# One sequence's start made on chip, another table of work for it, and fixed PSUM banks in a transformer block on one core

## What is computed

```python
xn = layernorm(x)
# attention: 16 heads of 16 channels, q = k = v = xn, causal
w = softmax(where(causal, q @ k.T / sqrt(16), min))
attn = w @ v
# ffn: lora rows from tokens 1..16 of the sequence itself
m1 = (even[:, :4, :, None] * odd[:, :4, None, :]).reshape(B, 1024, 256)
m2 = (even[:, 4:, :, None] * odd[:, 4:, None, :]).reshape(B, 256, 1024)
h = gelu(xn @ W1.T + scale * (xn @ m1.T) + b1)
ffn = h @ W2.T + scale * (h @ m2.T) + b2
out = x + attn + ffn
```

## Time and profile before

| | |
|---|---|
| median of 3 runs | 940.79 us (940.0 to 941.72) |
| profiled execution | 942.08 us |
| its span | 940.3 us |
| TensorE matmul busy | 855.6 us (91%) |
| ScalarE busy | 682.3 us (73%) |
| VectorE busy | 621.6 us (66%) |
| GpSimd busy | 185.3 us (20%) |
| chain that ended last | TensorE 72%, ScalarE 16%, VectorE 4%, DMA 2% |

### The profile page before, as it was taken

The page is one execution under the profiler, slowest core; times in us unless marked ns, Lnnn a source line. Parts: engine busy times, 40 slices in busy tenths (PEclk is TensorE's granted clock), DMA queues, the critical chain, the costliest instruction groups (busy, mean ns, idle before and its releaser), DMA issues.

```text
span 940.3 us, 17554 instructions
## 1 busy us (share of the span) xinstructions
PE 855.6 (91%) x7040; PEld 485.9 (52%) x7040; DVE 621.6 (66%) x1260; ACT 682.3 (73%) x737; POOL 185.3 (20%) x264
## 2 busy tenths in 40 slices
PE   1689999999999999999999999999999999999994
PEld 1255645656465554646446564555646555465642
DVE  7876695767677596675957668576767759562511
ACT  0547688777878778776887778777787877878782
POOL 1202122120312213121221212212121211212120
PEclk9989999999999999999999999999999999999998
DMA  4845436462373723555353633646246383313113
GB/s 134 298 137 169 144 101 192 130 184 74 102 213 113 241 64 114 145 167 187 102 164 84 203 123 103 191 139 175 73 114 201 114 241 91 107 35 93 38 12 101
DMA packets 212145, 127.18 MB, mean 135 GB/s; under 512 B 139168, under 2 KB 180320, under 8 KB 211040
## 3 DMA queue, kind: packets, MB, share of 16 engines
q1 hardware_dynamic: 212064, 126.06, 45.6%
HBM read 84.02 MB, written 42.01 MB: 134 GB/s over the span
## 4 chain that ended last, share of the span: by engine, by line
PE 72%; ACT 16%; DVE 4%; DMA 2%; issue 2%; POOL 2%; SPq 1%; DVEq 0%; ACTq 0%
PE o_ps L458 27%; PE work L486 15%; PE work L473 14%; PE scores L438 14%; ACT probs L394 13%; ACT L404 2%; POOL probs L386 2%; PE work L498 2%; ACT gelu L404 1%; DMA even<-even_dram 1%; DVE acc L670 1%; DVE xt_w L632 1%; DVE w_lo L599 1%; DMA q_dram<-xt_pair 0%; DMA xn<-x 0%
## 5 line engine op out<-in xcount | busy, mean ns | idle before, releaser
L394 ACT ACTIVATE probs<-scores 128x1024 f32<-128x1024 f32 x576 | 553.5, 1025 | 160.1 <-PE scores L438 159.9
L386 POOL TENSOR_SCALAR_AFFINE_SELECT probs<-probs 128x512 f32<-128x512 f32 x256 | 182.8, 732 | 735.6 <-ACT probs L394 735.6
L458 PE MATMUL o_ps<-probs,v_ones 128*32 128x512 f32 (+3 forms) x3072 | 281.0, 493 | 1.8 <-POOL probs L386 1.7
L438 PE MATMUL scores<-q_stack,k_stack 64*128 64x512 f16 (+3 forms) x1536 | 187.6, 331 | 28.2 <-ACT probs L394 19.3
L486 PE MATMUL work<-w_hi,g_hi 128*128 128x256 f32 x512 | 156.0, 305 | 0.0
L458 PEld LDWEIGHTS o_ps<-probs,v_ones 128*32 128x32 f32 x3072 | 84.1, 109 | 134.4 <-issue 106.6
L486 PE MATMUL work<-w_lo,g_hi 128*128 128x256 f32 x512 | 146.0, 285 | 0.0
L486 PE MATMUL work<-w_hi,g_lo 128*128 128x256 f32 x512 | 145.8, 285 | 0.0
L404 ACT ACTIVATE gelu<-work,b_sb 128x512 f32<-128x512 f32 x128 | 86.5, 688 | 79.2 <-PE work L473 73.4
L438 PEld LDWEIGHTS scores<-q_stack,k_stack 64*128 64x128 f16 x1536 | 51.9, 94 | 164.3 <-ACT probs L394 121.1
L473 PE MATMUL work<-xt_hi,w_hi 128*128 128x512 f32 x256 | 104.9, 410 | 17.4 <-ACT gelu L404 17.4
(11 more groups left out here) (41 smaller groups left out, 543.9 us busy)
## 6 DMA issues: line engine op xcount, KB each, us to landing
q_stack<-q_dram SPq DMA_DIRECT2D x32, 512.0 KB, 4.9
k_stack<-k_dram SPq DMA_DIRECT2D x64, 256.0 KB, 5.2
q_dram<-xt_pair SPq DMA_DIRECT2D x30, 512.0 KB, 4.6
xn<-x SPq DMA_DIRECT2D x16, 512.0 KB, 5.3
w<-w1t SPq DMA_DIRECT2D x8, 1024.0 KB, 7.8
even<-even_dram SPq DMA_DIRECT2D x8, 1024.0 KB, 5.1
xt_w<-w2t SPq DMA_DIRECT2D x8, 1024.0 KB, 5.8
acc<-x SPq DMA_DIRECT2D x8, 1024.0 KB, 7.0
```

The lines of the kernel that those rows point to most:

```text
L386: pool.affine_select(out=blk, in_=blk, compare_op=ALU.is_ge, fill=0.0, base=0, pattern=[[0, GH], [1, P]], channel_multiplier=-1).then_inc( ...
L394: act.activation(probs[:, slot % RING, 2 * half:2 * half + 2, :].rearrange("p h q -> p (h q)"), scores[:, half, :], ACT.Exp, scale=EXP_SCA ...
L438: last = pe.matmul(scores[:, half, h * BANK + at:h * BANK + at + n], k_stack[rows, g % 2, half, kb * P:(kb + 1) * P], q_stack[rows, g % 2, ...
L458: last = pe.matmul(o_ps[VW * j:VW * (j + 1), half, q0 % BANK:q0 % BANK + n], v_ones[:, kb, GH * g + j, :], probs[:, slot % RING, j, at:at ...
```

## The change

For the first group of sequence 0 the stacks no longer go through DRAM. ScalarE (first half of the tokens) and GpSimd (second half) repeat each channel of xn four times along the free axis into `gelu`; TensorE transposes that (`spread_rows`) into the banks of `work` and `o_ps`; ScalarE writes a high fp16 part scaled by a column that is 1024 or 0 on alternating rows (`high_parts`, `low_rows`), and VectorE subtracts it (`boot_stacks`), so that a row holds either the low or the high part. GpSimd also normalises the second half of xn and copies V. The pair and the copies of xT follow in pieces (`boot_pair`, `boot_xt`), half of them in pair 0, and m1, m2 and their splits move into pairs 1 to 4 of sequence 0.

Sequence 0 has its own tables, with FFN1 first in pair 4 instead of 1. The other sequences have fewer FFN2 passes in pairs 5 to 7, the second FFN1 in pair 10 instead of 9, and some VectorE steps one to three pairs elsewhere. FFN2 and later transposes have fixed banks: FFN2 bank 0, transposes bank 1, FFN1 alternates. On SP's queue w1, w2 and acc are loaded first, and the even rows are stored once half of xn is there.

```diff
 BETWEEN = {
     2: [("ffn2", 0, 0, 0, 12, 0)],
-    10: [("ffn2", 1, 0, 0, 12, 0)],
+    11: [("ffn2", 1, 0, 0, 12, 0)],
 }
...
-    5: [("ffn2", 0, 2, 0, 12, 0), ("xn", 0)],
-    6: [("ffn2", 0, 2, 12, 24, 0), ("xn", 1)],
-    7: [("ffn2", 0, 3, 0, 12, 0), ("xn", 2)],
-    8: [("ffn2", 0, 3, 12, 24, 0), ("xn", 3)],
-    9: [("ffn1", 1)],
-    10: [("ffn2", 1, 0, 12, 24, 0)],
-    11: [("ffn2", 1, 1, 0, 8, 0)],
-    12: [("ffn2", 1, 1, 8, 16, 0)],
-    13: [("ffn2", 1, 1, 16, 24, 0)],
+    5: [("ffn2", 0, 2, 0, 8, 0), ("xn", 0)],
+    6: [("ffn2", 0, 2, 8, 16, 0), ("xn", 1)],
+    7: [("ffn2", 0, 2, 16, 24, 0), ("xn", 2)],
+    8: [("ffn2", 0, 3, 0, 12, 0)],
+    9: [("ffn2", 0, 3, 12, 24, 0)],
+    10: [("xn", 3), ("ffn1", 1)],
+    11: [("ffn2", 1, 0, 12, 24, 0)],
+    12: [("ffn2", 1, 1, 0, 12, 0)],
+    13: [("ffn2", 1, 1, 12, 24, 0)],
...
+FIRST_BETWEEN = {
+    12: [("ffn2", 1, 0, 0, 12, 0)],
+}
+FIRST_BEHIND = {
+    4: [("ffn1", 0)],
+    6: [("ffn2", 0, 0, 0, 24, 0)],
+    7: [("ffn2", 0, 1, 0, 24, 0)],
+    8: [("ffn2", 0, 2, 0, 12, 0), ("xn", 0)],
+    9: [("ffn2", 0, 2, 12, 24, 0), ("xn", 1)],
+    10: [("ffn2", 0, 3, 0, 24, 0), ("xn", 2)],
+    11: [("xn", 3), ("ffn1", 1)],
+    12: [("ffn2", 1, 0, 12, 24, 0)],
...
+}
...
-LN_STATS, LN_RSTD, LN_APPLY, ADD_B2 = 2, 3, (3, 4), (7, 12)
-SCALE_ODD, ADD_M1, SPLIT_XT, SPLIT_M1, ADD_M2, COPY_V, SPLIT_M2 = 8, 9, 10, 11, 14, 16, 0
+LN_STATS, LN_RSTD, LN_APPLY, ADD_B2 = 2, 3, (3, 4), (7, 9)
+SCALE_ODD, ADD_M1, SPLIT_XT, SPLIT_M1, ADD_M2, COPY_V, SPLIT_M2 = 10, 10, 11, 12, 15, 16, 0
...
+BOOT_XT, BOOT_ADD_M1, BOOT_SPLIT_M1, BOOT_ADD_M2, BOOT_SPLIT_M2 = 0, 1, 2, 3, 4
...
         if piece not in bank:
-            bank[piece] = turn if kept is None else 1 - kept
...
+            first_use = what == "xn" and key[0] == 0
+            at = key[2] % 2 if what == "ffn1" else key[1] % 2 if first_use else int(what == "xn")
+            bank[piece] = at, had[at]
...
@@ SyncE @@
             load_x(0)
+            load_w1()
...
-            load_w1()
-            sp.wait_ge(xn_ready, 1)
-            store_even(0)
-            sp.wait_ge(pair_ready, 1)
-            store_heads(0, 0, GH, group0_out)
-            sp.wait_ge(group0_out, 16 * STORE_DMAS)
-            load_stacks(0, 0)
-            load_even(0)
-            sp.wait_ge(xt_split, 1)
             load_w2()
             load_acc(0)
...
+            sp.wait_ge(xn_half_ready, 1)
+            store_even(0)
+            load_even(0)
+            sp.wait_ge(pair_ready, 1)
+            store_heads(0, GH, HEADS // DT - GH, pair_out[0])
+            sp.wait_ge(pair_out[0], 16 * STORE_DMAS)
             load_stacks(0, 1)
+            sp.wait_ge(pair_ready, DT)
+            store_heads(0, HEADS // DT, HEADS // DT, pair_out[1])
...
@@ GpSimd @@
+            pool.wait_ge(rstd_ready, 1)
+            for t in range(NT // 2, NT):
+                ins = pool.tensor_scalar(xn[:, t, :], xn[:, t, :], mean_var[:, t, 0:1], rstd[:, t, :],
+                                         ALU.subtract, ALU.mult)
+            ins.then_inc(xn_ready, 1)
+            pool.wait_ge(xn_ready, 1)
+            for u in range(GH // 2):
+                pool.wait_ge(spread, u + 1)
+                to, dims = dims_repeated(u, 1)
+                pool.tensor_copy(to, dims).then_inc(repeated[1], 1)
...
@@ ScalarE @@
+            def high_parts(half):
+
+                for u in range(GH // 2):
+                    k = GH // 2 * half + u
+                    act.wait_ge(spread, k + 1)
+                    if k >= 2:
+                        act.wait_ge(boot_stacked, 2 * k - 2)
+                    for which in range(2):
+                        act.activation(high[k % 2][:, which, :], spread_bank(u, half), ACT.Identity,
+                                       scale=low_rows[:, which:which + 1]).then_inc(high_made, 1)
+
...
+            high_parts(0)
             exps(0)
+            high_parts(1)
             exps(1)
...
@@ TensorE @@
             pe.wait_ge(ident_made, 1)
-            for u in range(XT_USES):
+            for half in range(2):
+                for u in range(GH // 2):
+                    spread_rows(u, half)
+            scores_of(0)
+            for u in range(2):
                 transpose_xn(0, u)
-            scores_of(0)
             scores_of(1)
...
+                    if b == 0 and p == 0:
+                        for u in range(2, XT_USES):
+                            transpose_xn(0, u)
...
@@ VectorE @@
+            boot_rows()
             ln_stats(0)
             ln_rstd()
+            dve.sem_inc(rstd_ready, 1)
             ln_apply(0, xn_half_ready)
...
+            boot_stacks(0)
+            boot_pair(0)
+            boot_stacks(1)
+            boot_pair(1)
             dve.wait_ge(consts_in, 32)
...
+            for u in range(2):
+                boot_xt(u)
...
+                        if p == BOOT_XT:
+                            for u in range(2, XT_USES):
+                                boot_pair(u)
+                            for u in range(2, XT_USES):
+                                boot_xt(u)
+                            dve.sem_inc(xt_split, 1)
+                            add_b2(0, 0)
+                            add_b2(0, 1)
+                        if p == BOOT_ADD_M1:
+                            add_m1(0)
+                        if p == BOOT_SPLIT_M1:
+                            split_m1()
+                        if p == BOOT_ADD_M2:
+                            add_m2(0)
+                        if p == BOOT_SPLIT_M2:
+                            split_m2()
```

More of the change, by code:

```diff
@@ L105, in work_of @@
 def work_of(table, b, p):
+    if b == 0:
+        table = FIRST_BETWEEN if table is BETWEEN else FIRST_BEHIND
     for what, *arg in table.get(p, ()):
@@ L126, in _uses @@
         if piece not in bank:
-            bank[piece] = turn if kept is None else 1 - kept
[L128 to L133, removed]
+            first_use = what == "xn" and key[0] == 0
+            at = key[2] % 2 if what == "ffn1" else key[1] % 2 if first_use else int(what == "xn")
+            bank[piece] = at, had[at]
+            had[at] += 1
+        if what != "ffn2" or key[4] == FFN2_PASSES:
             end[piece] = len(end)
@@ L196, in attention_ffn @@
         ident = sb("ident", [P, P])
+        low_rows = sb("low_rows", [P, 2])
         b1_sb = sb("b1_sb", [P, MT])
@@ L223, in attention_ffn, with dims_repeated, spread_bank @@
         chain = sem("chain")
+        def dims_repeated(u, half):
+            dims = xn[:, TB * half:TB * (half + 1), 2 * HD * u:2 * HD * (u + 1)]
+            return (gelu[:, u, :].rearrange("p (t c r) -> p t c r", t=TB, r=4),
+                    dims.unsqueeze(3).broadcast_to([P, TB, 2 * HD, 4]))
+        def spread_bank(u, half):
+            return o_ps[:, u, :] if half else work[:, u, :]
         block = ctx.enter_context(nc.Block())
@@ L429, in scores_of @@
                 b, g, i = slot // SEQ, slot // NS % GROUPS, slot % NS
-                if i == 0:
-                    pe.wait_ge(stacks_in[g % 2], 16 * STACK_DMAS * (2 * b + g // 2 + 1))
+                if i == 0 and slot:
+                    pe.wait_ge(stacks_in[g % 2], 16 * STACK_DMAS * (2 * b + g // 2 + g % 2))
                 for half in range(2):
+                    if slot < NS:
+                        pe.wait_ge(boot_stacked, 2 * (half + 1) if slot < 2 else 2 * (GH // 2 + half + 1))
                     if 2 * slot + half >= 2:
@@ L454, in times_v @@
                         pe.wait_ge(masked, masks)
-                    if kb == 0 and slot >= NS:
-                        pe.wait_ge(o_evac[half], GROUPS * b + g)
+                    if kb == 0:
+                        if slot >= NS:
+                            pe.wait_ge(o_evac[half], GROUPS * b + g)
+                        else:
+                            pe.wait_ge(boot_stacked, 4 * (GH // 2))
                     for j in range(GH):
@@ L491, in transpose_xn @@
             def transpose_xn(b, u):
[L492 to L495, removed]
+                if b == 0 and u < 2:
+                    pe.wait_ge(boot_stacked, 2 * (u + 1))
+                pe.wait_ge(xn_ready, b + 1)
                 bank = bank_for("xn", b, u)
@@ L500, in transpose_xn, with spread_rows @@
                 last.then_inc(work_ready, 1)
-            pe.wait_ge(ident_made, 1)
-            for u in range(XT_USES):
+            def spread_rows(u, half):
+                pe.wait_ge(repeated[half], u + 1)
+                for t in range(TB):
+                    last = pe.transpose(spread_bank(u, half)[:, P * t:P * (t + 1)], gelu[:, u, P * t:P * (t + 1)],
+                                        ident[:, :])
+                last.then_inc(spread, 1)
+            pe.wait_ge(ident_made, 1)
+            for half in range(2):
+                for u in range(GH // 2):
+                    spread_rows(u, half)
+            scores_of(0)
+            for u in range(2):
                 transpose_xn(0, u)
-            scores_of(0)
```

(27 more changed lines are left out.)

88 lines of the change are left out of this document (43 added, 45 removed), and 5 rows, old and new, of the table FIRST_BEHIND.

## The result

The changed kernel takes 929.79 us (929.03 to 930.45, four runs) against 940.39 of the kernel before beside it: a ratio of 0.9885, interval 0.9867 to 0.9902, 1.15% faster. The forecast was 917.3 with a range of 909 to 925: the kernel is 12.5 us slower than that, and of the 23.5 us that the change was to bring 10.6 came. The profiled execution's span is 928.7 us.

A forecast was written before the change was run, and what follows sets the result against it. ScalarE's exps set a 4.61 us floor per pair; bank waits and the start lay above it. Later sequences 16.2 plus start 7.3 made 23.5 us off, 917.3 us as a median, range 909 to 925.

The forecast's parts named there:

- The start's sum: Sequence 0: FFN1's tile 4 at 57.8 us, 5.2 later for three pairs more (13.8); start's gain 7.3 us.
- The rest of sequence 0: Sequence 0 around its pairs: blocks, passes and transposes cost 7.9 us after against 6.6 before, a loss of 1.3.
- The gain of the banks: Later sequences, pairs whose transposes wait for FFN2's bank: wait gone and pair back at 4.61 us, 1.25 saved.
- The 0.50 that I withheld in pair 5: Later sequences, pair 5: transposes would wait for the normalised x, so its 0.50 us gain was not counted.
- The moved VectorE steps: Later sequences: odd, m1, m2 and b2 keep their durations and stay pairs ahead of their users; no cost.
- the contention with the selects for pair 11: Later sequences: block moved before a two-mask slot, GpSimd's selects late beside VectorE; 0.2 us a sequence, 1.2 over six.
- The clock: Sequence 0, FFN1's second half: clock falls behind a 3 us idle, so it costs 8.45 us, 2.8 lost.
- Rival 2: Sequence 0, pairs without FFN work: TensorE stays at 1.2 GHz, +5 us, 922; chance 0.13.
- Rival 3: The start: on-chip stacks don't move its end, since VectorE, repeats, table loads or GpSimd add up; gain 0, 924.6; chance 0.14.
- Rivals 1: FFN1 and pair 5: clock holds (2.8 us) and normalised x comes in time (3.0), 911.5; chance 0.15.
- the single bank: FFN2's 64 blocks: each would wait some 0.68 us for VectorE's addition, 43.5 in all, 961; chance 0.04.
- Rival 5: Later sequences: moved passes do nothing as ScalarE's floor is higher; only the start's 7.3 us remains, 933.5; chance 0.04.

The follow-up runs named there:

- e1: Changed kernel with sequence 0's store of o (group 0, second half) put before SP's wait for the next normalised x: 923.77 us, ratio 0.9822.
- f1: e1 with the later sequences' tables and step pairs put back as before; fixed banks, start and first table as changed: 924.4 us, ratio 0.9824.
- f2: e1 with both b2 additions of the later sequences in pair 7: 920.64 us, ratio 0.9782.
- e3: The kernel before with the fixed banks alone, tables and start as before: 928.54 us, ratio 0.9871.
- f3: f2 with the addition of o's second half in pair 5 instead of 2: 914.64 us, ratio 0.972.
- f4: f3 with VectorE instead of GpSimd normalising the second half of sequence 0's x in the start: 912.18 us, ratio 0.9693.
- e2: Changed kernel with the second b2 addition of the later sequences back in pair 12 instead of 9: 933.46 us, ratio 0.9924.

## Why the prediction was wrong

*The start's sum.* Up to FFN1 it held within 1.3 us: tile 4 resumed at 59.09 for a forecast of 57.8. The first scores began at 18.81 where I had them complete at 18.8, 1.0 us late in all, and for another reason than I gave: not VectorE's stacks, but the transposes of the second half, which waited 1.47 us for GpSimd. FFN1 could start 2 us late, as the second part of W1's split took 3.37 beside GpSimd's selects instead of 2.50, and m2 took 4.64 instead of 5.51. The step that failed stands in the change's second part, "The rest of sequence 0", where I added only passes and transposes of TensorE, 7.9 against 6.6, and took the work of the other queues as unchanged. I had looked at SP's queue for the later sequences ("their users are several pairs behind. Nothing.") and not for sequence 0, where the norm steps move from pairs 2 to 4 to pairs 5 to 7 and one store of o is left behind that wait. The waits and e1 show its price: 5.7 us of the 6.6 that were missing at the mark. With the queue mended the mark lies 0.1 us from the forecast in e1 and 0.7 in f1 and f2. The 0.1 is in part luck: in e1 tile 4 stood 0.4 late, FFN1's second half took 1.1 less than the 8.45 that I let it cost, and the rest up to the mark 0.6 more.

*The later sequences.* The gain of the banks was right, 1.25 for a pair with such a wait, of which 0.86 by the bank, as e3 shows. The 0.50 that I withheld in pair 5 was right too: six waits of 0.35 for the normalised x, worth 0.49 each when they went (f3). What failed is "The moved VectorE steps (odd, m1, m2, b2) have the same durations and remain ahead of their users by pairs". One of them, b2 in pair 9, stands in front of GpSimd's selects (0.66 a sequence: the period of f2 against e1's), and the splits a pair later leave VectorE late for the evacuation in pair 13. In sequence 2 the pairs behind the second FFN1 take 0.45 more than in e3, for a recorded wait of 0.2. The 0.45 is still there in f4, and no run took it away, so that this cause is read from the traces only. I had named the contention with the selects for pair 11 and priced it at 0.2 a sequence; it did not come there, and came in pair 10. Together the two take back 1.1 of the 1.2 us a sequence that the fewer passes gave, so that the tables net to nothing (f1).

*The clock.* I let it fall behind FFN1's idle of 3 us and cost 2.8. The idle was 2.4. In the profiled execution of the change the granted clock stayed at 1.00 in all of FFN1 (5.79 us for 24 passes) and fell behind it, to 0.63 from 71 to 73 us; in e1 it fell to 0.53 inside FFN1, from 59 to 61. The term measured some 1.5 us in either place. Rival 2, the slow level in pairs 1 to 3, is out: P·V takes 1.93 us there from 32.8 on. Rival 3, a start that gains nothing, is what one sees in the end, but its reason was not: the work up to FFN1's tile 4 came out only 1.3 us over its cost, and between the table load at 0.80 us and the one at 51.09 there is none.

Rivals 1, 4 and 5: the first did not come, since x is late in pair 5 and the clock fell one way or the other; the single bank costs nothing (e3); and the floor of 4.61 us is real, pairs 6 to 8 keep it. Rival 5's 933.5 was also added up wrongly: had the moved passes done nothing, the banks would still have given their 1.7 us a sequence. In the later sequences that is close to what came (1.8), for another reason.

The parts add up to the result: 12.2 us for the banks (e3), nothing for the later tables (f1), 4.1 for the start and its table with the store in its place (f1 against e3), less 5.7 for the store: 10.6.

## What to carry to other kernels

When a table moves a step, walk every in-order queue that waits for that step, in the first iteration too, and list what stands behind the wait in each. The loss here was a store of o that had nothing to do with the norm but came after it in SP's program. And judge a part of a change alone: one part of four, the banks, carried more than the whole.

## What the runs showed of the hardware

Two selects of GpSimd (128 x 512) take 2.2 us where a VectorE addition with both inputs in SBUF runs beside them, behind pair 2 (and 2.20 in the changed kernel) and in pair 9; where the addition was moved away, they took 1.22 in the same places (f3 behind pair 2, e2 in pair 9). The Trainium skill's "SBUF — State Buffer" (Who interferes with whom) gives exclusive use of a shared port pair as the reason, and these times agree with it.

GpSimd took 5.01 us for four tensor_scalars of 128 x 256 with two scalars per partition, 1.23 for the last, beside which VectorE was idle, where VectorE takes 0.33 each (2.67 for eight in f4). Its plain copies of 128 x 512 took 0.6 each, and VectorE's copy of that size out of PSUM 0.69. So it is nearly four times as slow in the one and no slower in the other. I had bounded it by twice VectorE's time.

The change of ScalarE between Identity and Exp loads no table: the two alternate from 12.72 us on, and no load stands between 0.80 and 51.09. The Trainium skill's "ScalarE: Activation LUTs" (Table sets) says that identity is in every set, and the trace agrees.

A short wait in front of a matmul can cost more than its length: 0.86 us of the pair for 0.68 (e3), 0.45 for 0.24 and 0.49 for 0.35 (f3).
